# Layer 0 and 1 of a two-layer attention kernel: normalized tile written by ScalarE, a token-major feed-forward, mixing in three operations, stores two steps apart

## The chip, the cores and the metric

The kernel runs on one core of one Trainium2 chip. The metric is device time in microseconds, the median of several executions. Engines are named as in the profile: PE (TensorE matmul) and PEld (its weight loads), DVE (VectorE), ACT (ScalarE), POOL (GpSimd), SP (SyncE, which here only issues DMAs).

## The reference, cut to what matters

Two residual layers over x of shape (16, 512, 128), float32. Only layer 0's feed-forward branch and the normalization in front of both layers are touched.

```
xn = layernorm(x)                      # (x - mean) / sqrt(var + 1e-5), both layers
x  = x + attn(xn) + ffn(xn)            # 16 heads of 8, causal in layer 0

# ffn of layer 0
x_prev = concat([zeros, xn[:, :-1, :]])
xr = mu_r * xn + (1 - mu_r) * x_prev
xk = mu_k * xn + (1 - mu_k) * x_prev
r  = sigmoid(xr @ W_r.T)
out = r * (square(relu(xk @ W_k.T)) @ W_v.T)
```

## The kernel before, in words

One batch is 512 tokens, four tiles of 128 (NT = 4). Each layer is a software pipeline over the 16 batches, written as "bodies". A body has 64 slots: four groups u of heads, in each four key tiles kt, in each four tiles j (slot = 16u + 4kt + j). Every engine runs the same bodies in the same slot order with its own instructions, in order, and engines meet only through semaphores. First layer 0's bodies run alone, then three bodies of layer 0 and three of layer 1 interleaved slot by slot, then layer 1's alone.

In a slot PE makes transposed scores of one head and key tile (`scores_t`, L646, ring 0 of three PSUM banks), which ACT exponentiates into `probs` (L941), and the scores for the row maxima of a later group (`scores_max`, L667 and L671, mask added in L683; ring 1 of four PSUM banks), which DVE reduces into `maxs` (L1151 to L1182). At each kt, POOL masks (layer 0, L1290) or multiplies a bias (layer 1, L1316) on `probs`, and PE multiplies them with the values (`pv`, L630). POOL splits the maxima in two bf16 parts (`split_max`, L1299, L1301), PE transposes them (uses MT0 to MT3, L701), ACT copies them out (L839) and SP sends them as a row into the score operands (`stacks`, L506), which the next group's scores_t waits for.

All other work is put into slots by the hand-written tables `WORK_USES` (uses of a PSUM bank: slot of PE's part, slots later at which it is taken out, batch offset) and `OTHER_WORK` (slot, batch offset). A use claims the next bank of its ring in order and waits until the bank's last content has been taken; the names in `BY_DVE` use ring 1, all others ring 0. The parts that matter here:

- LN, slot 3: DVE takes bn_stats and bn_aggr of `x_tile` (L1064, L1068), adds eps (L1070). POOL makes `rstd` with pow one slot later (L1247).
- NORM, slot 7 in layer 0 and 18 in layer 1: DVE writes `xn` = (x - mean) * rstd, four operations (L1074). XT, slot 14 or 21: PE transposes xn (L707), ACT writes `xnT` (L842).
- MIX, slot 2, layer 0: DVE makes `fa` and `fb`, the two mixtures of `xnT` and `xnT` shifted by a token, two operations each (L1083, L1085).
- FR, slot 6, and FK, slot 9: PE multiplies W_r with fa and W_k with fb (L714), channels on the partitions. ACT takes tanh into `fc` (L851), relu into `fd` (L854). POOL squares fd (L1251).
- FV, slot 15: PE multiplies W_v with fd (L718); DVE takes it out a slot later as (fc + 1) * FV into fa (L1090). FT, slot 35: PE transposes fa back to tokens (L730); ACT scales it by 0.5 into `ffn` (L870).
- POST, slot 21: POOL adds residual, attention and `ffn` into `x_new` (L1256, L1258). STORE, slot 26 (layer 0) or 34 (layer 1): POOL moves the row indices on (L1230) and issues four indirect DMAs in a row (L1238).
- PJ0 to PJ3 project xnT to queries, keys and values (L724, L860); SQUARE, MEAN (slot 35), ROOT (slot 38) and SCALE_QK (slot 43) are the RMS norm of queries and keys (ACT L874 and L877, DVE L1094 to L1103). ACT loads another table for the square root and one to get back (L877, L941). QT (slot 47) and KT (slot 59) transpose q and k (L740); they are stored in parts (L533).
- SP, in order: at u = 0 the row of MT0, then the residual, then 24 loads of `stacks` from `parts_scratch` (L479; in layer 1 12 of them at u = 0 and 12 at u = 1, behind MT1); at u = 2, behind MT2, the next x_tile; at u = 3, behind MT3, the stores of parts. The maxima of the next body's first group, from slot 32 on, need the 24 loads.

Of the kernel before, what the change touches and what calls it, by code (L numbers as in the profile page):

```python
# [14 lines left out]
ALU = mybir.AluOpType  # L15
# [3 lines left out]
P = 128  # L19
NB, T, D = 16, 512, 128  # L20
H, HD = 16, 8
NT = T // P
# [31 lines left out]
BOTH = 3  # L54
ST_BANKS, MAX_BANKS = 3, 4
# [48 lines left out]
def place(layer, kt, j):  # L104

    if layer == 1:
# [20 lines left out]
    0: {"MIX": (2, 1), "LN": (3, 2), "NORM": (7, 2), "VALUES": (15, 1), "POST": (21, -1),  # L127
        "STORE": (26, -1), "SQUARE": (32, 2), "MEAN": (35, 2), "ROOT": (38, 2), "SCALE_QK": (43, 2)},
    1: {"LN": (3, 2), "NORM": (18, 2), "BESIDE": (22, -1), "STORE": (34, -1)},
# [174 lines left out]
def build(nc, a, out):  # L304
# [14 lines left out]
    with ExitStack() as ctx:  # L319
# [36 lines left out]
        rstd = sb("rstd", [P, NT])  # L356
        sqr = sb("sqr", [P, NT, 2 * P])
# [18 lines left out]
        mu = sb("mu", [P, 4])  # L376
# [180 lines left out]
        def _(pe):  # L557
# [39 lines left out]
            def body(B):  # L597
# [89 lines left out]
                def other(slot):  # L687
# [21 lines left out]
                    if layer == 0:  # L709
                        for n, name in enumerate(("FR", "FK")):  # L710
                            if B.due(name, slot):
                                work = claim(name)
# [13 lines left out]
                        if B.due("FT", slot):  # L726
                            work = claim("FT")
# [3 lines left out]
                            last.then_inc(full, 1)  # L731
# [81 lines left out]
        def _(act):  # L813
# [8 lines left out]
            def body(B):  # L822
# [8 lines left out]
                def other(slot):  # L831
                    u = slot // 16
                    mo, mu_ = (u + 1) // NG, (u + 1) % NG
                    if B.out(f"MT{u}", slot):
# [4 lines left out]
                        fn(mT[:], work[0:2 * G * NT, 0:P // 2].bitcast(BF16), ACT.Copy).then_inc(taken, 1)  # L839
                    if B.out("XT", slot):  # L840
# [7 lines left out]
                    if layer == 0:  # L848
# [17 lines left out]
                        if B.out("FT", slot):  # L866
                            work = filled("FT")
                            if B.has(-1):
                                act.wait_ge(s["post"], B.count(2, 2, -1))
                            fn(ffn[:, B.parity(1)].rearrange("p t d -> p (t d)"), work, ACT.Copy, scale=0.5  # L870
                               ).then_inc(taken, 1)
# [85 lines left out]
        def _(dve):  # L957
# [49 lines left out]
            def before_second_body():  # L1007
# [4 lines left out]
                v.tensor_scalar(mu[:, 2:4], mu[:, 0:2], -1.0, 1.0, ALU.mult, ALU.add).then_inc(rep_chain, 1)  # L1012
                dve.wait_ge(rep_chain, 5)

            def after_second_body():
# [5 lines left out]
                dve.wait_ge(rep_chain, 6)  # L1021
# [3 lines left out]
            def body(B):  # L1025
# [13 lines left out]
                def other(slot):  # L1039
# [21 lines left out]
                    if B.due("LN", slot):  # L1061
# [7 lines left out]
                        link(last, "ln", 3, 2, 2)  # L1069
# [132 lines left out]
        def _(pool):  # L1202
# [13 lines left out]
            def body(B):  # L1216
# [25 lines left out]
                def other(slot):  # L1242
                    if B.due("STORE", slot):
                        store()
# [130 lines left out]
```

## Time and profile before

| | us |
|---|---|
| three runs, median (lowest to highest) | 1820.95 (1817.0 to 1830.35) |
| the profiled execution, its own time | 1825.96 |
| its span, first to last instruction | 1824.1 |
| mean granted TensorE clock | 0.943 of full |
| busy over the span | PE 1606.0, DVE 1445.2, ACT 1287.8, POOL 932.1 |

Layer 0 alone runs steadily from about 120 to 826 us, both layers interleaved to about 1000 us, layer 1 alone to the end. The busy times are sums over stages with different limits. "PEclk" in the windows is the granted share of TensorE's full clock; a window half of which ran at the lower level shows 0.75. A row of windows gives the stretch, its length, the busy time of PE, PEld, DVE, ACT and POOL with their instruction counts, PEclk, the DMA share and GB/s.

### The profile page before, as it was taken

To read this page: it belongs to the slowest core of one execution; us is meant where nothing else is said; L and a number is where in the kernel's file an instruction comes from. 1 tells how busy PE (TensorE), PEld (TensorE's weight loads), DVE (VectorE), ACT (ScalarE), POOL (GpSimd) and SP (SyncE) were. 2 spreads that over 40 slices of the span, in tenths; PEclk is the share of its full clock that TensorE was granted. 3 is DMA by queue.
4 is the path that set the end of the run, shared out by engine and by line. 5 is a ranking of instruction groups with operands and counts; after the bars stand their busy time and mean duration, and the time that the engine had idled before them with its cause. 6 is when DMAs were issued, how large, how long until landed. Compare 5 with 4: busy or idle time off the path is not lost.

```text
span 1824.1 us, 32723 instructions
## 1 busy us (share of the span) xinstructions
PE 1606.0 (88%) x11594; PEld 621.3 (34%) x11594; DVE 1445.2 (79%) x2571; ACT 1287.8 (71%) x2502; POOL 932.1 (51%) x1144
## 2 busy tenths in 40 slices
PE   4798898888888888889879999999999999999995
PEld 2453333333333333333323233232332323323231
DVE  4358778787877878878878888888888888898881
ACT  1227777666766666777667788877888888887885
POOL 2123545554455444555455565555665556564555
PEclk9759989898999989999989999999999999999999
DMA  8313323222223222213232222322222222222200
GB/s 269 58 35 65 71 58 70 55 64 69 71 71 65 70 67 70 71 47 78 63 56 59 55 56 56 59 59 54 56 50 65 59 61 57 54 54 59 60 18 18
DMA packets 133122, 116.36 MB, mean 64 GB/s; under 512 B 16856, under 2 KB 125664, under 8 KB 132960
## 3 DMA queue, kind: packets, MB, share of 16 engines
q1 hardware_dynamic: 126272, 100.64, 23.7%
q0 software_dynamic: 4096, 8.40, 1.4%
q10 hardware_dynamic: 2592, 5.24, 0.9%
q8 instruction: 93, 1.52, 0.3%
q14 instruction: 69, 0.57, 0.1%
HBM read 79.63 MB, written 33.55 MB: 62 GB/s over the span
## 4 chain that ended last, share of the span: by engine, by line
PE 55%; DVE 21%; ACT 10%; issue 4%; DMA 4%; SPq 2%; POOL 2%; another core or an unknown queue 0%; POOLq 0%; ACTq 0%; DVEq 0%
PE pv_acc L630 15%; PE scores_transposed L646 12%; ACT probs L941 5%; PE scores_transposed L774 4%; PE scores_for_max L667 3%; PE scores_transposed L724 3%; DMA stacks<-parts_scratch 3%; DVE maxs L1151 3%; DVE maxs L1178 3%; DVE maxs L1182 2%; DVE xn L1074 2%; PE scores_transposed L746 2%; PE scores_for_max L671 2%; PE scores_for_max L782 2%; PE scores_for_max L683 2%
## 5 line engine op out<-in xcount | busy, mean ns | idle before, releaser
L941 ACT ACTIVATE probs<-scores_transposed 128x512 f32<-128x512 f32 x1664 | 908.9, 600 | 234.7 <-PE scores_transposed L646 221.2
L646 PE MATMUL scores_transposed<-stacks 62*128 62x512 bf16 (+3 forms) x2048 | 575.4, 347 | 61.7 <-ACT probs L941 36.9
L1316 POOL TENSOR_TENSOR probs<-probs,near_bias 128x512 f32<-128x512 f32 x256 | 324.8, 1272 | 360.1 <-ACT probs L941 359.8
L630 PE MATMUL pv_acc<-probs,vals 128*32 128x512 f32 (+3 forms) x4096 | 485.4, 547 | 18.4 <-issue 9.7
L1151 DVE TENSOR_REDUCE maxs<-scores_for_max 128x2 f32<-128x1024 f32 x340 | 409.2, 1221 | 77.9 <-PE scores_for_max L667 75.7
L646 PEld LDWEIGHTS scores_transposed<-stacks 62*128 62x128 bf16 x2048 | 150.5, 94 | 625.6 <-ACT probs L941 298.1
L667 PE MATMUL scores_for_max<-stacks 60*128 60x512 bf16 x1024 | 324.6, 385 | 15.0 <-DVE maxs L1151 8.4
L671 PE MATMUL scores_for_max<-stacks 60*128 60x512 bf16 (+3 forms) x1024 | 262.4, 315 | 37.1 <-DVE maxs L1179 27.0
L1182 DVE TENSOR_REDUCE maxs<-scores_for_max 128x1 f32<-128x512 f32 x256 | 175.0, 684 | 90.8 <-PE scores_for_max L683 79.4
L1154 DVE TENSOR_REDUCE maxs<-scores_for_max 128x1 f32<-128x512 f32 x344 | 226.4, 684 | 25.7 <-PE scores_for_max L667 23.0
L1290 POOL TENSOR_SCALAR_AFFINE_SELECT probs<-probs 128x512 f32<-128x512 f32 x256 | 166.9, 667 | 139.1 <-ACT probs L941 138.6
L1178 DVE TENSOR_REDUCE maxs<-scores_for_max 128x1 f32<-128x384 f32 x256 | 140.3, 548 | 70.3 <-PE scores_for_max L683 60.0
L683 PE MATMUL scores_for_max<-causal_halves,ident_halves 64*128 64x128 bf16 (+2 forms) x1280 | 193.3, 237 | 0.0
L630 PEld LDWEIGHTS pv_acc<-probs,vals 128*32 128x32 f32 x4096 | 82.8, 110 | 179.9 <-issue 135.8
L683 PEld LDWEIGHTS scores_for_max<-causal_halves,ident_halves 64*128 64x128 bf16 x1280 | 115.2, 99 | 39.3 <-issue 7.2
L1222 POOL TENSOR_TENSOR parts<-rest,parts 128x512 bf16<-128x512 f32 x64 | 75.4, 1178 | 67.0 <-ACT parts L917 67.0
L671 PEld LDWEIGHTS scores_for_max<-stacks 60*128 60x128 bf16 x1024 | 76.8, 95 | 56.0 <-DVE maxs L1179 32.9
L1173 DVE TENSOR_REDUCE maxs<-scores_for_max 128x2 f32<-128x512 f32 x128 | 87.4, 683 | 8.0 <-PE scores_for_max L683 7.0
L667 PEld LDWEIGHTS scores_for_max<-stacks 60*128 60x128 bf16 x1024 | 73.6, 93 | 41.1 <-DVE maxs L1151 24.3
L746 PE MATMUL scores_transposed<-xnT,w 128*128 128x512 f32 x128 | 78.9, 701 | 9.2 <-ACT probs L941 7.7
L1247 POOL TENSOR_TENSOR rstd<-mv,minus_half 128x4 f32<-128x4 f32 x32 | 40.2, 1256 | 71.5 <-DVE mv L1070 71.5
L1238 POOL DMA_INDIRECT out_dram<-x_new,slots_now x64 | 63.0, 985 | 23.8 <-issue 14.8
(129 smaller groups left out, 2031.4 us busy)
## 6 DMA issues: line engine op xcount, KB each, us to landing
stacks<-parts_scratch SPq DMA_DIRECT2D x768, 64.0 KB
parts_scratch<-parts SPq DMA_DIRECT2D x64, 384.0 KB, 2.6
x_tile<-in_L_attn_x_dram SPq DMA_DIRECT2D x16, 256.0 KB, 2.8
probs<-in_fc_B_dram ACTq DMA_DIRECT2D x1, 4096.0 KB, 19.1
stage_a<-in_fc_A_T_dram SPq DMA_DIRECT2D x1, 4096.0 KB, 16.9
stacks<-mT SPq DMA_DIRECT2D x256, 4.0 KB
x_res<-in_L_attn_x_dram SPq DMA_DIRECT2D x16, 256.0 KB, 3.6
x_tile<-x_between_layers SPq DMA_DIRECT2D x16, 256.0 KB
```

Of the source, the lines that this page charges most:

```text
L630: last = mm(acc[VW * j:VW * j + VW, q0:T], columns[:, first:first + VW], probs[:, row, column:column + width], start=(kt == 0 and pu % PAI ...
L646: last = mm(st[:, bank, column:column + T - q0], ks[p][rows, h, P * kt:P * kt + P], qs[p][rows, h, q0:T], start=True, stop=True)
L667: mm(bank, qs[p][rows, h, P * qt:P * qt + P], ks[p][rows, h, :], start=True, stop=True).then_inc(s["s1_ready"], 1)
L671: mm(bank[:, column:column + P * (qt + 1)], qs[p][rows, h, P * qt:P * qt + P], ks[p][rows, h, 0:P * (qt + 1)], start=True, stop=False, ski ...
L683: last = mm(masked, ident_halves[half, n, :], mask, start=False, stop=(n == 1), skip_group_check=True)
L941: fn(probs[:, row, :], st[:, B.use(("st", u, number)).bank, :], ACT.Exp, scale=SCALE).then_inc(s["exp_done"], 1)
L1151: v.reduce_max(maxs[:, su % 2, :].rearrange("p (e x) -> p e x", e=E)[:, :, column], s1[:, bank - 1:bank + 1, :], AX_X).then_inc(s["red_don ...
L1154: v.reduce_max(maxs[:, su % 2, column:column + 1], s1[:, bank, :], AX_X).then_inc(s["red_done"], 1)
L1178: v.reduce_max(maxs[:, su % 2, wide:wide + 1], bank[:, 0:3 * P], AX_X)
L1182: v.reduce_max(maxs[:, su % 2, column:column + 1], bank, AX_X).then_inc(s["red_done"], 1)
L1290: g.affine_select(out=diag, in_=diag, compare_op=ALU.is_ge, fill=0.0, base=0, pattern=[[0, G], [1, P]], channel_multiplier=-1).then_inc(s[ ...
L1316: g.tensor_tensor(diag, diag, near_bias[:, kt, :].unsqueeze(1).broadcast_to([P, G, P]), ALU.mult).then_inc(s["emul_pool"], 1)
```

## The change

The normalized tile is written by ACT as Identity(scale * x + bias), with scale = rstd and bias = -mean * rstd. DVE negates the mean, POOL multiplies it with rstd. NORM moves to slot 11 (layer 0) and 19 (layer 1). MIX becomes one difference into `fd` and one fused operation each for fa and fb; `mu` loses its two complement columns. FR and FV put the tokens on the partitions by using fa and fd as the stationary operand, in four matmuls of 128 columns each; so FT and its copy are gone, DVE writes `ffn` directly, and FV moves from slot 15 to 35. The factor 0.5 goes into W_v once, at set-up. Layer 0's OA is taken out a slot later, MT1 moves from slot 19 to 21; in layer 1 MT0 moves from 4 to 6, XT from 21 to 20, MT2 from 35 to 43. The four indirect stores are issued two slots apart in both layers. The diff, cut to its core:

```
+STORE_STEPS = 2
 WORK_USES = {
-    0: {"MT0": (2, 0, 0), "FR": (6, 0, 1), "FK": (9, 0, 1), "XT": (14, 0, 2), "FV": (15, 0, 1),
-        "OA": (16, 0, -1), "MT1": (19, 0, 0), ... "FT": (35, 0, 1), ...
-    1: {... "MT0": (4, 0, 0), ... "XT": (21, 0, 2), ... "MT2": (35, 0, 0), ...
+    0: {"MT0": (2, 0, 0), "FR": (6, 0, 1), "FK": (9, 0, 1), "XT": (14, 0, 2), "OA": (16, 1, -1),
+        "MT1": (21, 0, 0), ... "FV": (35, 0, 1), ...
+    1: {... "MT0": (6, 0, 0), ... "XT": (20, 0, 2), ... "MT2": (43, 0, 0), ...
 OTHER_WORK = {
-    0: {... "NORM": (7, 2), ...     1: {... "NORM": (18, 2), ...
+    0: {... "NORM": (11, 2), ...    1: {... "NORM": (19, 2), ...
@@ PE
-        for n, name in enumerate(("FR", "FK")):
-                pe.wait_ge(s["mix_done"], B.count(4, 2 * n + 2, 1))
-                mm(work, wrkv[:, n, :], (fa, fb)[n][:], start=True, stop=True).then_inc(full, 1)
+        if B.due("FR", slot):
+            pe.wait_ge(s["mix_done"], B.count(3, 2, 1))
+            for t in range(NT):
+                last = mm(work[:, P * t:P * t + P], fa[:, P * t:P * t + P], wrkv[:, 0, :], ...)
+        if B.due("FK", slot):
+            pe.wait_ge(s["mix_done"], B.count(3, 3, 1))
+            mm(work, wrkv[:, 1, :], fb[:], start=True, stop=True).then_inc(full, 1)
         if B.due("FV", slot):
-            mm(work, wrkv[:, 2, :], fd[:], start=True, stop=True).then_inc(full, 1)
+            for t in range(NT):
+                last = mm(work[:, P * t:P * t + P], fd[:, P * t:P * t + P], wrkv[:, 2, :], ...)
-        if B.due("FT", slot):
-            taken_out("FV")
-            for t in range(NT):
-                last = tr(work[:, P * t:P * t + P], fa[:, P * t:P * t + P], ident[:])
@@ ACT
+        if B.due("NORM", slot):
+            act.wait_ge(s["pow_ln"], B.count(2, 2, 2))
+            for t in range(NT):
+                fn(xn[:, t, :], x_tile[:, t, :], ACT.Identity, scale=rstd[:, t:t + 1],
+                   bias=shift[:, t:t + 1]).then_inc(s["xn_done"], 1)
-        if B.out("FT", slot):
-            fn(ffn[:, B.parity(1)]..., work, ACT.Copy, scale=0.5).then_inc(taken, 1)
@@ DVE
+        v.tensor_scalar(mv[:, :, 0], mv[:, :, 0], -1.0, None, ALU.mult)
         v.tensor_scalar(mv[:, :, 1], mv[:, :, 1], LN_EPS, None, ALU.add).then_inc(s["ln"], 1)
-        for t in range(NT):
-            v.tensor_scalar(xn[:, t, :], x_tile[:, t, :], mv[:, t, 0:1], rstd[:, t:t + 1], ...)
         if B.due("MIX", slot):
+            link(v.tensor_tensor(fd[:], xt[:, 1:T + 1], xt[:, 0:T], ALU.subtract), "mix_done", 3, 1, 1)
             for n, mix in enumerate((fa, fb)):
-                link(v.tensor_scalar(mix[:], xt[:, 1:T + 1], mu[:, n:n + 1], None, ALU.mult), ...)
-                v.scalar_tensor_tensor(out=mix[:], in0=xt[:, 0:T], scalar=mu[:, 2 + n:3 + n], in1=mix[:], ...)
+                v.scalar_tensor_tensor(out=mix[:], in0=fd[:], scalar=mu[:, n:n + 1], in1=xt[:, 0:T], ...)
         if B.out("FV", slot):
-            v.scalar_tensor_tensor(out=fa[:], in0=fc[:], scalar=1.0, in1=work, op0=ALU.add, op1=ALU.mult)
+            dve.wait_ge(s["post"], B.count(2, 2, -1))
+            v.scalar_tensor_tensor(out=ffn[:, B.parity(1)]..., in0=fc[:], scalar=1.0, in1=work, ...)
@@ POOL
+    for t in range(NT):
+        if B.after("STORE", slot, STORE_STEPS * t):
+            store_rows(t)
     if B.after("LN", slot, 1):
         g.tensor_tensor(rstd[:], mv[:, :, 1], half[:, 0:NT], ALU.pow).then_inc(s["pow_ln"], 1)
+        pool.wait_ge(s["pow_ln"], B.count(2, 1, 2))
+        g.tensor_tensor(shift[:], mv[:, :, 0], rstd[:], ALU.mult).then_inc(s["pow_ln"], 1)
@@ set-up, DVE
-    v.tensor_scalar(mu[:, 2:4], mu[:, 0:2], -1.0, 1.0, ALU.mult, ALU.add)
+    v.tensor_scalar(wrkv[:, 2, :], wrkv[:, 2, :], 0.5, None, ALU.mult)
```

## Rows read from the trace of the kernel before

**Rows 1.** DVE timeline: first token-mixing instruction of the batches at 169 and 813 us.
```profile
169.44 0.76 DVE L1083 TENSOR_SCALAR fa<-xnT,mu 128x512 f32<-128x512 f32 x1
...
812.66 0.77 DVE L1083 TENSOR_SCALAR fa<-xnT,mu 128x512 f32<-128x512 f32 x1
```

**Rows 2.** Windows: one steady layer 0 stretch, then both layers, then layer 1 (PEclk is 1.00 at full clock).
```profile
413.90:512.84 98.94, 86.41 (x756) 37.09 (x756) 78.75 (x174) 68.40 (x126) 50.52 (x75) 0.93 0.24 66
...
826.00:1000.00 174.00, 152.34 (x1084) 56.72 (x1088) 143.00 (x243) 121.77 (x244) 84.51 (x107) 0.92 0.30 64
1000.00:1824.10 824.10, 753.66 (x4833) 250.79 (x4825) 688.37 (x993) 655.10 (x1322) 471.17 (x494) 0.98 0.23 53
```

**Rows 3.** Waits of PE, 150 to 800 us (layer 0): total us, times, longest.
```profile
PE scores_for_max L671 <- DVE maxs L1179: 26.3, 27, 1.5
PE scores_transposed L701 <- POOL msp L1301: 15.2, 20, 1.1
PE scores_transposed L646 <- ACT probs L941: 11.3, 7, 1.7
...
PE pv_acc L630 <- POOL probs L1290: 5.9, 13, 0.5
```

**Rows 4.** Critical chain, 455 to 512 us: start, us, what.
```profile
464.76 0.70 DVE fa L1083
...
466.91 0.75 DVE fb L1085
...
470.92 2.42 DVE xn L1074 x4
...
475.98 1.95 PE scores_for_max L718 x2
...
489.49 0.74 issue
```

**Rows 5.** Windows around the three drops of the granted clock in two batches.
```profile
421.00:431.00 10.00, 8.48 (x50) 3.30 (x44) 6.48 (x14) 3.38 (x7) 2.82 (x6) 0.66 0.39 120
449.00:455.00 6.00, 5.00 (x34) 2.24 (x34) 3.75 (x8) 4.41 (x9) 4.34 (x6) 0.72 0.01 3
471.00:481.00 10.00, 8.03 (x62) 3.53 (x61) 7.83 (x18) 4.64 (x10) 3.59 (x7) 0.83 0.56 119
```

**Rows 6.** Groups by line: busy us, mean ns, idle before.
```profile
L1074 DVE TENSOR_SCALAR xn<-x_tile,mv,rstd 128x128 f32<-128x128 f32 x128 | 65.5, 638 | 2.3 <-POOL rstd L1247 2.3
L905 ACT ACTIVATE ffn<-scores_transposed 128x128 f32<-128x128 f32 x64 | 17.8, 278 | 17.2 <-PE scores_transposed L774 17.2
L730 PE MATMUL scores_transposed<-ident,fa 128*128 128x128 f32 x64 | 11.0, 296 | 0.0
L764 PE MATMUL scores_transposed<-wqkv,xnT 128*128 128x128 f32 x128 | 19.5, 297 | 0.0
L1090 DVE SCALAR_TENSOR_TENSOR fa<-fc,scores_for_max 128x512 f32<-128x512 f32 x16 | 11.0, 685 | 16.0 <-PE scores_for_max L718 16.0
L1230 POOL TENSOR_TENSOR slots_now<-slots_now,a_batch 128x4 int32<-128x4 int32 x30 | 5.9, 197 | 0.0
L877 ACT ACT_TABLE_LOAD x16 | 20.5, 1283 | 0.3
```

**Rows 7.** Timelines of POOL and DVE, batch of 462 us: stores, a mask, means.
```profile
484.65 1.07 POOL L1238 DMA_INDIRECT x_between_layers<-x_new,slots_now  x1 [0.29 <-POOL slots_now L1230]
...
489.52 0.65 POOL L1290 TENSOR_SCALAR_AFFINE_SELECT probs<-probs 128x512 f32<-128x512 f32 x1
...
493.76 1.21 DVE L1094 TENSOR_REDUCE ssq<-sqr 128x128 f32<-128x1024 f32 x1
```

**Rows 8.** Waits of PE, 826 to 1000 us (both layers), then 1000 to 1700 (layer 1).
```profile
PE scores_transposed L707 <- DVE xn L1074: 6.0, 2, 3.3
...
PE scores_transposed L646 <- ACT probs L941: 14.4, 46, 0.6
```

**Rows 9.** Critical chain, 1155 to 1212 us (layer 1).
```profile
1164.05 7.78 DMA stacks<-parts_scratch
```

More of the change, by code:

```diff
@@ L126 @@
 OTHER_WORK = {
-    0: {"MIX": (2, 1), "LN": (3, 2), "NORM": (7, 2), "VALUES": (15, 1), "POST": (21, -1),
+    0: {"MIX": (2, 1), "LN": (3, 2), "NORM": (11, 2), "VALUES": (15, 1), "POST": (21, -1),
         "STORE": (26, -1), "SQUARE": (32, 2), "MEAN": (35, 2), "ROOT": (38, 2), "SCALE_QK": (43, 2)},
-    1: {"LN": (3, 2), "NORM": (18, 2), "BESIDE": (22, -1), "STORE": (34, -1)},
+    1: {"LN": (3, 2), "NORM": (19, 2), "BESIDE": (22, -1), "STORE": (34, -1)},
 }
@@ L356, in build @@
         rstd = sb("rstd", [P, NT])
+        shift = sb("minus_mean_rstd", [P, NT])
         sqr = sb("sqr", [P, NT, 2 * P])
@@ L375, in build @@
         wrkv = sb("wrkv", [P, 3, P])
-        mu = sb("mu", [P, 4])
+        mu = sb("mu", [P, 2])
         normw = sb("normw", [P, 2, HD])
@@ L709, in other @@
                     if layer == 0:
-                        for n, name in enumerate(("FR", "FK")):
-                            if B.due(name, slot):
-                                work = claim(name)
-                                pe.wait_ge(s["mix_done"], B.count(4, 2 * n + 2, 1))
-                                mm(work, wrkv[:, n, :], (fa, fb)[n][:], start=True, stop=True).then_inc(full, 1)
+                        if B.due("FR", slot):
+                            work = claim("FR")
+                            pe.wait_ge(s["mix_done"], B.count(3, 2, 1))
+                            for t in range(NT):
+                                last = mm(work[:, P * t:P * t + P], fa[:, P * t:P * t + P], wrkv[:, 0, :],
+                                          start=True, stop=True)
+                            last.then_inc(full, 1)
+                        if B.due("FK", slot):
+                            work = claim("FK")
+                            pe.wait_ge(s["mix_done"], B.count(3, 3, 1))
+                            mm(work, wrkv[:, 1, :], fb[:], start=True, stop=True).then_inc(full, 1)
                         if B.due("FV", slot):
@@ L717, in other @@
                             pe.wait_ge(s["kact_done"], B.count(1, 1, 1))
-                            mm(work, wrkv[:, 2, :], fd[:], start=True, stop=True).then_inc(full, 1)
+                            for t in range(NT):
+                                last = mm(work[:, P * t:P * t + P], fd[:, P * t:P * t + P], wrkv[:, 2, :],
+                                          start=True, stop=True)
+                            last.then_inc(full, 1)
                         for t in range(NT):
@@ L865, in other @@
                                ).then_inc(s["vals_done"], 1)
-                        if B.out("FT", slot):
[L867 to L871, printed above, removed]
                         if B.due("SQUARE", slot):
@@ L1069, in other @@
                         link(last, "ln", 3, 2, 2)
+                        v.tensor_scalar(mv[:, :, 0], mv[:, :, 0], -1.0, None, ALU.mult)
                         v.tensor_scalar(mv[:, :, 1], mv[:, :, 1], LN_EPS, None, ALU.add).then_inc(s["ln"], 1)
-                    if B.due("NORM", slot):
-                        dve.wait_ge(s["pow_ln"], B.count(1, 1, 2))
-                        for t in range(NT):
-                            v.tensor_scalar(xn[:, t, :], x_tile[:, t, :], mv[:, t, 0:1], rstd[:, t:t + 1],
-                                            ALU.subtract, ALU.mult).then_inc(s["xn_done"], 1)
                     for side, name in enumerate(("QT", "KT")):
@@ L1236, in store, with store_rows @@
                         pool.wait_ge(s["dve_taken"], B.use("PR").taken[1])
-                    for t in range(NT):
-                        g.indirect_dma_start(x_dst[layer],
-                                             bass.IndirectOffsetOnAxis(slots_now[:, layer, t:t + 1], 0),
-                                             x_new[:, t, :], None).then_inc(s["x_stored"], 16)
+                def store_rows(t):
+                    g.indirect_dma_start(x_dst[layer], bass.IndirectOffsetOnAxis(slots_now[:, layer, t:t + 1], 0),
+                                         x_new[:, t, :], None).then_inc(s["x_stored"], 16)
                 def other(slot):
```

16 lines of the change are left out of this document (5 added, 11 removed), and 12 rows, old and new, of the table WORK_USES.

## The prediction

> **What bounds the kernel now.** I read the views in this order: the windows by stage, the waits of PE, the critical chain of one layer 0 batch, the granted clock in fine windows, then the groups by line for prices.
>
> The windows split the span in three. In layer 0 no engine is full: over two batches PE is busy 86.41 of 98.94 us, DVE 78.75, at a mean granted clock of 0.93. In layer 1 PE is busy 753.66 of 824.10 us at 0.98, so it is close to its limit [rows 2]. So layer 0 has the room. Its period is (812.66 - 169.44) / 13 = 49.48 us a batch [rows 1].
>
> The waits say who makes PE stand: in 13 batches 26.3 us for maxima that DVE had not reduced, 15.2 us for split maxima, 11.3 us for exponentials, 5.9 us for POOL's masks [rows 3]. The chain shows where: DVE is on it from 464.76 to 467.66 us with the mixing, and with the four operations that write `xn`, 2.42 us; as soon as these are through, PE transposes xn and then runs FV, two passes in 1.95 us [rows 4]. That FV is slow because the granted clock falls right there: half the clock, 1.2 GHz of the two levels 1.2 and 2.4, follows the stretch in which PE stood waiting for DVE. The reader is to see three drops in two batches: 0.66 over 10 us, 0.72 over 6 and 0.83 over 10, that is 2 x (1 - clock) x length = 6.8, 3.4 and 3.4 us at half clock [rows 5]. The first and third follow the `xn` stretch, the second the pair of table loads for the root.
>
> **The change part by part**, against the profiled execution (1825.96 us, of which 1824.1 span; the median of the runs is 5.0 lower). Layer 0 has 13 full batches between 169 and 813 us.
>
> *NORM to ACT, layer 0.* DVE loses 2.42 us on the chain [rows 4] and gets one small operation, at most 0.2 us by the nearest small row, POOL's 128x4 [rows 6]. POOL gets one more of that size plus a wait on itself, 0.3 us; behind it in POOL's order is the mask that pv at slot 12 waits for, a wait of 5.9 / 13 = 0.45 us now [rows 3]. DVE reaches LN earlier by what mixing saves (0.5 or more, below), so that mask comes 0 to 0.45 us earlier: I take 0.3. The longest single wait of PE on DVE is 1.5 us, once a batch, right behind `xn` [rows 3]; DVE arrives about 3 us earlier there, so it goes. Sum 1.8 us. ACT pays: an activation of 128x128 takes 278 ns [rows 6], four of them at most 1.1 us with nothing overlapped and 0.6 if starts overlap; I take 0.85. It lies at slot 11, ahead of XT at 14, and behind it in ACT's queue stand the exponentials of slot 12 and the copy of pv_acc that pv at slot 16 waits for. ACT is busy 68.40 of 98.94 us [rows 2], and 4.64 of 10 us around this place [rows 5], so I cost it at nothing; without that cover it is 0.85 a batch. What is late next is XT itself: LN, pow, shift, four activations end within some 0.1 us of when PE can be there.
>
> *The clock.* With the stand gone, the drops behind it should go: 10.2 us at half clock in two batches [rows 5], 5.1 a batch, of which half is lost, 2.55 us. PE is the one waited for in most of it. Bounds 0 and 2.55; I take 2.0, since one of the drops may move to another stand instead of going.
>
> The Trainium skill has a rule against this ("TensorE: Matmul & The Clock Gate", section Part 4: PE-mode transpose): transposes do not count as work for the clock. By it the four of XT would leave the clock low whatever precedes them, and this term would be 0. The drop that follows the table loads has no such transposition in front, which speaks for the idle time; no row separates the two at XT. It is the first rival.
>
> *MIX in three.* 2.9 us now for four operations [rows 4]; three, at 0.69 (a fused one of this size, L1090 [rows 6]) to 0.8 each, are 2.1 to 2.4: 0.5 to 0.8 less. It is inside the same DVE backlog as `xn` and already spent there; nothing of its own.
>
> *FR and FV by tokens, FT away.* Four f32 matmuls of 128 columns cost 19.5 us / 16 = 1.22 a batch (the layer 1 row L764), the one of 512 columns 1.95 / 2 = 0.98 at full clock [rows 4, 6]. So each of the two pays 0 to 0.24 more. FT's four transposes go, 11.0 / 16 = 0.69 us of PE [rows 6], and its copy on ACT, about 0.5. FV leaves the stretch where PE is the bound (1 us at full clock) and comes to slot 35, in front of the only long stand of PE that remains, that for ACT's table loads (11.3 us in 7 cases, up to 1.7 us [rows 3]). Bounds 0.2 and 1.2; I take 0.6.
>
> *FV on DVE.* The operation is the same, 685 ns, and loses its idle time of 1 us in front at slot 16 [rows 6], which was not the bound. At slot 36 it stands directly behind MEAN, 1.21 us plus two more [rows 7], and holds one of four ring 1 banks meanwhile; reductions behind it, and SCALE_QK and QT after them, come up to 0.6 us later. Cost 0 to 0.8, taken 0.6.
>
> *Stores two slots apart.* They block POOL from 484.65 to the mask at 489.52 us [rows 7], and PE stands 0.74 us until that mask is done [rows 4]. The mask can now run after the first of them: a gain of 0 to 0.74, taken 0.7. The other three, 1.3 us each, lie between later masks; the fourth, at slot 32, is behind the split of maxima and not in front of it. OA and MT1 one and two slots later have slack of ten slots, no cost.
>
> Together 1.8 + 2.0 + 0.6 - 0.6 + 0.7 = 4.5 us a batch, 13 batches: 58.5 us.
>
> *Both layers, 826 to 1000 us.* XT waited 6.0 us for `xn` in two places [rows 8]. ACT, less laden there than DVE (121.77 against 143.00 us [rows 2]), should end most of it: 4 us, bounds 0 and 6.
>
> *Layer 1.* DVE loses at most (65.5 - 13 x 2.42) / 19 = 1.8 us a batch (what is left of the group [rows 4, 6], start-up included), ACT gets 0.85 at slot 19, in front of XT at slot 20. PE waits 14.4 us in 12 batches for exponentials [rows 8], so ACT matters as much as DVE. Moreover the 24 stack loads are on the chain: 7.78 us in one piece of DMA, issued behind MT1 at slot 17, which does not move, and needed at slot 32 [rows 9]. What is won between those slots is given back there. MT0 and MT2 later by 2 and 8 slots keep the five-slot lead that MT3 has. Bounds -8 and +8 over 14 batches; I take 1 us less.
>
> Sum: 58.5 + 4 + 1 = 63.5, so 1825.96 - 63.5 = 1762.5 for such an execution and 1820.95 - 63.5 = 1757.5 for the median.
>
> **The rivals.**
> *The clock stays low at XT.* For it: XT and idle time always come together in this trace. Against it: a batch has six groups of transposes (XT, OA, FT, QT, OB, KT), and two batches show three drops in all [rows 5]. Then the 2.0 us fall away: 2.5 x 13 + 5 = 37.5, giving 1783.
> *The wait moves.* XT waits for ACT instead of DVE, or the stack loads, which layer 0 also needs by slot 32, bind once the batch shortens by five. For it: pow, shift and NORM are a chain over three engines. Against: layer 0 issues all 24 loads at u = 0, sixteen slots ahead of layer 1's second half, and its waits show none of PE on them [rows 3]. Only some 1 us a batch remains, about 13 us and 0 to 5 more: 1806.
> *Slower: Identity needs a table of its own.* Then each of 32 NORMs costs ACT two loads of 1283 ns [rows 6] at slot 11 or 19. In layer 0 the present pair already makes PE stand up to 1.7 us [rows 3]; this eats the gain of 1.8 and keeps the clock low, leaving 0.7 x 13 = 9 us. In layer 1, with PE at 91%, a stand of 1.6 and a drop of 1.7 us in each of 14 batches are 46 us more: 1820.95 - 9 + 46 = 1858. It decides from one load in front of NORM on. Against: it is the root's line that has the 16 loads [rows 6], once a batch, though copies, squares and tanh come between the exponentials too. The Trainium skill ("ScalarE: Activation LUTs", Table sets: the hidden batching unit) says identity is in every set, and would give this case no time at all.
> *More than forecast.* All upper bounds, 5.9 a batch, and 14 in the rest: 1730.
>
> **How the numbers follow.** Forecast as stated (1736 to 1776) 0.60, more than forecast 0.08, clock stays low 0.17, the wait moves 0.10, slower 0.05. The range leaves out one in ten on each side: 1731 to 1800. A measurement here tells about 1% (18 us) from no change: faster by more 0.85, within 1% 0.10, slower 0.05.
>
> **What would show it.** The windows of layer 0: period 45 us instead of 49.5, mean clock 0.97 or more, one drop in two batches instead of three. In the waits, L671 on DVE from 26 to below 10 us, a small new one of L707 on ACT. No ACT_TABLE_LOAD on NORM's line. Layer 1's part of the span within 8 us of 824. The forecast is wrong if XT is followed by half clock as before, if L707 waits over 0.5 us a batch, or if the period stays above 47.

## The result, and the profile after

The changed kernel takes 1796.75 us (1790.92 to 1801.12, four runs) against 1821.31 us (four runs beside it): a ratio of 0.9857, 95% interval 0.9827 to 0.9888. It is faster by 24.6 us; the forecast was 63.5. Its median is within the range given, near the upper end, so the range held and the forecast did not. The profiled executions (1790.92 us, span 1789.2, against 1825.96, span 1824.1) are 35.0 us apart. The first lies 6 us below its median, the second 5 us above, so 10 us of that gap are scatter. Ratios leave out slow executions, those over 1.5% above the fastest of their kernel (three of ten in e9, three of six in e13, two of six in e17), and medians do not, so these three ratios are 0.3 to 0.7% lower than their medians say.

The windows of the changed kernel, over two of its batches, over the steady part of layer 0, around two drops of the clock, and around one XT (columns as in [rows 2]):

```profile
405.33:498.50 93.17, 83.42 (x780) 38.92 (x772) 73.42 (x165) 70.33 (x133) 52.59 (x77) 0.93 0.29 70
170.00:780.00 610.00, 543.22 (x5045) 252.59 (x5046) 478.96 (x1079) 458.93 (x863) 341.09 (x494) 0.94 0.29 70
434.00:444.00 10.00, 8.65 (x61) 4.11 (x61) 7.39 (x17) 6.83 (x14) 6.36 (x8) 0.66 0.00 0
480.00:490.00 10.00, 8.28 (x62) 3.58 (x62) 7.39 (x17) 6.59 (x12) 6.09 (x7) 0.66 0.00 0
411.00:421.00 10.00, 9.16 (x86) 4.13 (x87) 6.79 (x16) 8.23 (x18) 6.93 (x12) 1.00 0.57 117
```

The same 610 us of the kernel before:

```profile
170.00:780.00 610.00, 531.73 (x4647) 228.24 (x4643) 485.61 (x1068) 418.97 (x774) 308.84 (x453) 0.93 0.27 67
```

and of the run e2 below, the kernel before with NORM alone moved:

```profile
170.00:780.00 610.00, 539.13 (x4960) 236.23 (x4952) 485.91 (x1099) 464.97 (x879) 333.64 (x498) 0.97 0.28 70
```

The first row answers to the first of [rows 2]: two batches in 93.17 us instead of 98.94. PE is busy 83.42 instead of 86.41 us and stands 9.75 instead of 12.53. The clock is what did not follow: 0.93 in both pairs of batches, 0.94 against 0.93 over 610 us. The drops have changed their place. Both of the pair in the third and fourth row (0.66 over 10 us, 6.8 us at half clock each) lie behind the table loads of the root, where [rows 5] had one of three. None lies at XT any more: in the last row XT runs at full clock.

The timeline of DVE after gives the period, as [rows 1] did:

```profile
168.74 1.00 DVE L1083 SCALAR_TENSOR_TENSOR fa<-fd,mu,xnT 128x512 f32<-128x512 f32 x1
...
775.97 1.00 DVE L1083 SCALAR_TENSOR_TENSOR fa<-fd,mu,xnT 128x512 f32<-128x512 f32 x1
```

(775.97 - 168.74) / 13 = 46.71 us a batch against 49.48, where 45 was forecast. That is 2.77 x 13 = 36 us, all of the 35 us between the two profiled executions. The rest of the kernel, where 5 us were expected, gave nothing.

The waits of PE in layer 0 after, to be laid beside [rows 3]:

```profile
PE scores_transposed L648 <- ACT probs L945: 16.4, 15, 1.4
PE scores_transposed L703 <- POOL msp L1305: 15.5, 17, 1.1
PE scores_for_max L673 <- DVE maxs L1178: 11.6, 14, 1.0
PE scores_transposed L709 <- ACT xn L848: 10.9, 14, 1.4
...
PE scores_for_max L745 <- DVE big L1102: 6.1, 14, 0.8
PE scores_transposed L648 <- DMA stacks<-mT: 4.1, 1, 4.1
```

The wait for unreduced maxima is down from 26.3 to 11.6 us. Against it stand a new one, 10.9 us of XT on ACT's `xn`, and one that has grown, 6.1 us of QT on DVE's scaling (0.9 before, from 170 to 780 us). One batch stood 4.1 us for the row of maxima that SP sends behind MT1. The group of ACT's line 848 (busy us, mean ns, idle time before) and the critical chain at one NORM show why XT waits:

```profile
L848 ACT ACTIVATE xn<-x_tile,minus_mean_rstd,rstd 128x128 f32<-128x128 f32 x128 | 52.4, 484 | 0.1
```

```profile
410.66 0.59 ACT probs L945
411.25 1.53 ACT xn L848 x4
412.79 0.14 issue
412.92 0.63 PE scores_transposed L709 x4
```

One activation with two per-partition operands takes 484 ns, not the 278 it was priced at, and a NORM of four 52.4 / 32 = 1.64 us, not 0.85. PE is ready for XT at about 412.2 us and gets it at 412.9. And before QT, the timeline of DVE after:

```profile
429.36 0.69 DVE L1089 SCALAR_TENSOR_TENSOR ffn<-fc,scores_for_max 128x512 f32<-128x512 f32 x1 [0.27 <-PE scores_for_max L727]
429.96 1.21 DVE L1093 TENSOR_REDUCE ssq<-sqr 128x128 f32<-128x1024 f32 x1
...
435.40 1.22 DVE L1102 TENSOR_TENSOR big<-big,rrms 128x1024 f32<-128x1024 f32 x1
```

FV's operation with its wait (0.95 us) stands in front of MEAN here, not behind it: in its entry (35, 0, 1) the second number, 0, is the number of slots later, so it is taken out in its own slot 35. The same holds for the (15, 0, 1) of the kernel before: it was taken out in slot 15, not a slot later.

Layer 1's waits of PE, 1000 to 1700 us, beside [rows 8]:

```profile
PE scores_transposed L648 <- ACT probs L945: 11.7, 38, 0.6
PE scores_transposed L709 <- ACT xn L848: 10.6, 12, 0.9
```

ACT's exponentials hold PE a little less than before, but XT now waits 0.9 us in nearly every batch (12 waits). Before, PE had no wait for `xn` in the list of layer 1.

### The profile page after: what moved, and what is told of

It reads as the page before. It is cut to its first block, busy times and chain, and to the rows that moved or that the text cites. A ratio compares the mean times of both kernels' runs of the same rounds, so it can differ in the third digit from the quotient of the medians.

```text
span 1789.2 us, 32996 instructions
## 1 busy us (share of the span) xinstructions
PE 1579.5 (88%) x11722; PEld 631.3 (35%) x11722; DVE 1387.0 (78%) x2459; ACT 1326.8 (74%) x2614; POOL 952.5 (53%) x1176
## 3 DMA queue, kind: packets, MB, share of 16 engines
q1 hardware_dynamic: 126272, 100.64, 24.6%
## 4 chain that ended last, share of the span: by engine, by line
PE 61%; DVE 17%; ACT 11%; issue 4%; DMA 3%; POOL 2%; SPq 2%; POOLq 0%; ACTq 0%; DVEq 0%
PE pv_acc L632 17%; PE scores_transposed L648 14%; ACT probs L945 6%; PE scores_transposed L779 4%; PE scores_for_max L669 3%; PE scores_transposed L735 3%; DVE maxs L1150 3%; ACT xn L848 2%; PE scores_for_max L685 2%; PE scores_transposed L751 2%; PE scores_for_max L787 2%; PE scores_for_max L673 2%; PE scores_for_max L698 2%; DVE maxs L1181 2%; DVE maxs L1177 2%
## 5 line engine op out<-in xcount | busy, mean ns | idle before, releaser
L669 PE MATMUL scores_for_max<-stacks 60*128 60x512 bf16 x1024 | 328.3, 387 | 9.2 <-DVE maxs L1150 5.9
L673 PE MATMUL scores_for_max<-stacks 60*128 60x512 bf16 (+3 forms) x1024 | 257.2, 316 | 17.3 <-DVE maxs L1178 11.6
L1294 POOL TENSOR_SCALAR_AFFINE_SELECT probs<-probs 128x512 f32<-128x512 f32 x256 | 178.5, 710 | 159.9 <-ACT probs L945 159.6
```

Of the source, the lines that this page charges most:

```text
L669: mm(bank, qs[p][rows, h, P * qt:P * qt + P], ks[p][rows, h, :], start=True, stop=True).then_inc(s["s1_ready"], 1)
L673: mm(bank[:, column:column + P * (qt + 1)], qs[p][rows, h, P * qt:P * qt + P], ks[p][rows, h, 0:P * (qt + 1)], start=True, stop=False, ski ...
L1294: g.affine_select(out=diag, in_=diag, compare_op=ALU.is_ge, fill=0.0, base=0, pattern=[[0, G], [1, P]], channel_multiplier=-1).then_inc(s[ ...
```

## The experiments

Every run has its own executions of the kernel before beside it (medians 1819.5 to 1825.1), so the ratio is what is compared. "Period" is that of layer 0 as above; "layer 1" is the mean over twelve batches between copies of xnT (before 56.65 us, changed 56.92). Rows of waits are those of PE in the 610 us from 170 us on, unless said otherwise, with total, count and longest. "Half clock" is 2 x (1 - clock) x length over the same 610 us (before 85 us, changed 75). Period, layer 1, waits and half clock are those of the one profiled execution of each kernel. The half clock differs between executions of one kernel: over the whole span the four of e6 lie between 146 and 202 us.

**One part against the rest.**

`e1_norm_on_dve`: the changed kernel with the old NORM.

```
-        if B.due("NORM", slot):
-            act.wait_ge(s["pow_ln"], B.count(2, 2, 2))
...
+        if B.due("NORM", slot):
+            dve.wait_ge(s["pow_ln"], B.count(1, 1, 2))
...
```

> The changed kernel with NORM back on DVE at its old slots (7 and 18, XT at 21 in layer 1); all else stays changed. Theory A (the predicted terms): NORM on DVE costs a stand of 1.8 us and 2 us of clock a batch in layer 0, so about 1797 + 13 x 3 to 4 = 1836 to 1850. Theory B (XT now waits 0.8 us a batch for ACT in both layers, and the clock falls once a batch at the root's table loads anyway): layer 0 loses 1 to 1.5 us a batch, layer 1 wins 0.9 x 14: 1797 + 16 - 12 = about 1800, with the layer 1 wait of L709 gone.

Measured: 1808.62 us, ratio 0.9918 (0.9882 to 0.9954). Period 49.0, layer 1 56.3; PE waits 29.1 us for maxima again and never for xn.

`e2_norm_on_act_alone`: the same edit the other way round, on the kernel before.

> The kernel before with NORM alone moved to ACT (slots 11 and 19, XT at 20 in layer 1). Theory A: this carries 1.8 + 2.0 us a batch: 1821 - 50 = 1771. Theory B: it gives 1 to 1.5 us a batch in layer 0 and takes 0.9 in layer 1: 1810 to 1821. The four activations should take 1.64 us in one piece, as in the changed kernel.

Measured: 1800.85 us, ratio 0.9889 (0.9856 to 0.9922). Period 46.52, layer 1 57.0, half clock 41 us.

In the profiled executions NORM alone gives layer 0 all of its gain: 46.5 against 46.7 with everything. By the medians it gives most: e2's profiled execution is the fastest of its eight, 9 us below their median. NORM on ACT costs layer 1 some 0.3 us a batch (57.0 against 56.65), and putting it back wins 0.6 there (56.3 against 56.9). Theory A, the predicted terms, had 1836 to 1850 and 1771 and is out in both; theory B had the layer 1 side right, and its 1 to 1.5 us for layer 0 was too small (49.0 - 46.7 = 2.3, and 49.5 - 46.5 = 3.0).

`e9_feed_forward_alone`: the kernel before with FR and FV by tokens, FV at 35 and FT gone, as the change has them:

```
-        ..., "FV": (15, 0, 1), ... "FT": (35, 0, 1), ...
+        ..., "FV": (35, 0, 1), ...
```

> The kernel before with the token-major feed-forward alone: FR and FV by tokens, FV at 35, FT gone; NORM, mixing, stores and slots as before. As predicted it saves 0.6 us of PE a batch and costs 0.6 on DVE: period 49.5, total within 5 us of before. Theory D: FV on DVE in front of the sums makes PE wait at QT (L740 on DVE, 0.9 us in all before, now 5 or more), and less half clock is won than lost; PE's busy time at full clock falls by 0.7 to 0.9 us a batch. Total 1815 to 1821.

Measured: 1814.08 us, ratio 0.9921 (0.9878 to 0.9964), so 0.5% faster by the medians and 0.8% by the ratio, a little more than both theories allowed. Its period is 48.85, in an execution 9 us above the median. The wait for the scaling appears as theory D said:

```profile
PE scores_for_max L742 <- DVE big L1102: 4.4, 12, 0.6
```

Alone it is worth 0.8%, NORM alone 1.1%, and everything together 1.4%. The gains seem not to add, but the intervals are too wide to show it.

`e6_stores_in_a_row`, the changed kernel with

```
-STORE_STEPS = 2
+STORE_STEPS = 0
```

> The changed kernel with its four indirect stores issued one after the other again, at slots 26 and 34. If the predicted 0.7 us a batch is right: pv waits 0.7 us for the mask in layer 0 again, period 46.3 to 47.0, about 9 us more in all. If the freed time is given back at the next wait: period unchanged, total within 3 us.

Measured: 1792.28 us, ratio 0.9843 (0.9765 to 0.992), not distinguishable from the changed kernel. Period 46.49, also not longer, although pv's wait is back, now with no releaser found:

```profile
PE pv_acc L632 <- issue: 6.2, 13, 0.5
```

So a stand of 0.5 us a batch is there, where 0.7 was predicted. Whether removing it gains anything is not shown: the interval is 28 us wide and holds both no change and the 9 us of the forecast, and this execution has 31 us less at half clock than the changed kernel's.

**The clock and the stand before QT.** The root's operation was replaced in both kernels by one that needs no other table; the root itself is left out.

```
-                            fn(rrms[:], ssq[:], ACT.Sqrt).then_inc(s["root_done"], 1)
+                            fn(rrms[:], ssq[:], ACT.Tanh).then_inc(s["root_done"], 1)
```

`e3_changed_no_root_table`:

> The changed kernel with the square root of the RMS norm replaced by a tanh, so that the root itself is left out (wrong scale of queries and keys) and no second table is needed. Theory B (the pair of table loads makes PE stand and the clock falls behind it in every batch): two loads a batch of 1.28 us go, the drops behind them (5.1 us at half clock a batch) go: layer 0 period from 46.7 to 42 to 43, in all 1797 - 16 x 4 = 1733, clock in layer 0 0.99. Theory C (the clock falls wherever PE stands at all, here at XT): period 45, clock 0.95 or lower, in all about 1772.

`e4_before_no_root_table`:

> The kernel before with the same replacement (the root is left out). Theory B: the stretch of xn on DVE still makes the clock fall once a batch, so the gain is smaller than in the changed kernel: the table stand of about 1.6 and one drop of 3.4 in two batches: 1821 - 16 x 2.4 = 1783. If it gains as much as the changed kernel does, the two stands are independent of one another and theory B falls.

Measured: 1791.74 us, ratio 0.9805 (0.9734 to 0.9876), for the changed kernel, and for the one before 1821.79, ratio 1.0016 (0.9982 to 1.0051). Two loads a batch are worth nothing in the kernel before and little, if anything, in the changed one, whose intervals with and without them overlap (periods: changed 46.3, before 49.0). The wait has passed to the other engine, here in the changed kernel:

```profile
PE scores_for_max L745 <- DVE big L1102: 24.2, 13, 1.9
```

24.2 us in 13 batches for DVE's scaling, against 5.5 with the loads in place over the same stretch (in e4 22.3 in 12, against 0.9). PE stands before QT for two chains of about one length, ACT's loads and DVE's sums, reciprocal and scaling, so taking away one shows the other. Theory B's 1733 is far off.

`e11_root_on_pool` tried to shorten both: one power -0.5 on POOL for reciprocal, root and loads. `e12_root_on_pool_fv_52` has FV at slot 52 too.

```
-                            v.reciprocal(ssq[:], ssq[:]).then_inc(s["rms"], 1)
-                            fn(rrms[:], ssq[:], ACT.Sqrt).then_inc(s["root_done"], 1)
+                            g.tensor_tensor(rrms[:], ssq[:], half[:], ALU.pow).then_inc(s["root_done"], 1)
```

> The changed kernel with reciprocal (DVE), square root (ACT) and both table loads replaced by one power -0.5 on POOL. Theory F (PE stands before QT for two chains at once, ACT's table loads and DVE's FV, sums and reciprocal; only when both shorten does the stand shrink, which is why leaving out the root's table alone gave little): both stands go if POOL's 128x128 power takes 2 us or less: period 46.3 to about 43.5, half clock below 25 us, 1797 - 40 = 1757. If POOL needs 4 us or more, PE waits for the scaling instead and the total rises above 1797.

> As the run before, with FV at slot 52, so that DVE's chain in front of QT is 0.95 us shorter too. Theory F: a further 0.3 to 0.6 us a batch, 1750; if POOL's power is the bound, the same as the run before.

Measured: 2068.52 us (ratio 1.1379) and 2075.05 (1.1417).

The group of the new line in e11:

```profile
L1251 POOL TENSOR_TENSOR rrms<-ssq,minus_half 128x128 f32<-128x128 f32 x16 | 333.0, 20812 | 90.9 <-DVE ssq L1093 90.9
```

The power of 128x128 takes 20.8 us. In both, pv waits up to 20.2 us at a time for masks queued behind it. Theory F, that the stand shrinks only when both chains do, stays untested.

**Where FV stands.** `e5_fv_at_29`, the changed kernel with

```
-        "MT2": (32, 0, 0), "FV": (35, 0, 1), ...
+        "FV": (29, 0, 1), "PJ3": (31, 0, 2), "MT2": (32, 0, 0), ...
```

> The changed kernel with FV at slot 29 instead of 35, a stretch in which PE is full and DVE stands idle for 1 to 1.4 us at a time. Theory D (in the changed kernel FV's operation on DVE, 0.95 us with its wait, stands in front of the sums, the reciprocal and the scaling of q and k, and PE waits for those at QT, 5.5 us in 13 batches, with the clock falling behind it): the wait of L745 on DVE goes, the half clock in layer 0 (75 us) falls to about 40, period 46.5 to 45.5, in all about 12 to 15 us less. Rival E (place of FV does not matter, PE's sum of work does): period unchanged at 46.3.

Measured: 1797.1 us, ratio 0.985 (0.9794 to 0.9906): no change. The wait of QT on DVE is gone from the list, but half clock rose to 82 us and the period to 47.6. Theory D had its wait right and its gain wrong. The clock falls at XT again, in 11 of 13 batches, 37.5 us in all, here once:

```profile
468.00:478.00 10.00, 10.00 (x71) 3.90 (x71) 5.45 (x13) 6.37 (x13) 5.76 (x9) 0.83 0.39 99
```

Yet XT's transposes and its wait for ACT (9.6 us in 13) are those of the changed kernel, in which no drop lies there.

**How long NORM sits on ACT.** The next runs change that piece or what waits for it. `e7_xt_later`:

```
-"XT": (14, 0, 2)   (layer 0)      "XT": (20, 0, 2)   (layer 1)
+"XT": (17, 0, 2)                  "XT": (22, 0, 2)
```

> The changed kernel with XT three slots later in layer 0 (17) and two later in layer 1 (22). NORM on ACT takes 1.64 us, twice what was predicted, and PE waits 0.74 us in layer 0 and 0.8 in layer 1 a batch for it. Theory B: both waits go, 0.7 x 13 + 0.8 x 13 = 20 us less, 1777. Rival: ACT's 1.64 us delay its exponentials, and the wait comes back as one of L648 on ACT: total unchanged.

Measured: 1789.07 us, ratio 0.9785 (0.9702 to 0.9868), period 46.9, layer 1 56.4. In layer 0 the rival holds: XT no longer waits, and pv waits for masks instead, twice a batch; POOL makes them from ACT's exponentials, which stand behind NORM in ACT's queue:

```profile
PE pv_acc L632 <- POOL probs L1294: 20.8, 26, 1.1
```

That is 20.8 us against 6.2 in the changed kernel over the same stretch. In layer 1, 0.5 us a batch came, though XT still waits there (10.1 us in 12, now for exponentials). `e8_fv_at_52_xt_later` adds `"FV": (52, 0, 1)` in place of `(35, 0, 1)`:

> The changed kernel with XT later as in the run before and FV at slot 52, far behind the scaling. If theories B and D both hold, their gains add: 20 + 12 to 15 us less than the changed kernel, about 1763, half clock in layer 0 at 40 us or below.

Measured: 1787.59 us, ratio 0.9789 (0.9731 to 0.9848), the same again. Half clock was 48 us, not the 40 or below that was expected, and the time was 25 us above the expectation.

`e10_norm_one_operation` leaves the normalization out (a plain copy under the same name) and measures its price; `e15_norm_four_plain` keeps the four operations and drops only scale and bias:

```
-                        for t in range(NT):
-                            fn(xn[:, t, :], x_tile[:, t, :], ACT.Identity, scale=rstd[:, t:t + 1],
-                               bias=shift[:, t:t + 1]).then_inc(s["xn_done"], 1)
+                        fn(xn[:], x_tile[:], ACT.Identity).then_inc(s["xn_done"], NT)
```

> The changed kernel with NORM as one ACT operation of 128x512 that only copies x (the normalization itself is left out): about 0.63 us instead of 1.64. Theory B (the size of NORM on ACT is what PE waits for at XT, 0.74 and 0.8 us a batch): L709's wait falls to below 0.1 us a batch in both layers, about 0.7 x 29 = 20 us less, 1777. Rival: the loop closes elsewhere and less than 8 us comes of it.

> The changed kernel with its four activations without scale and bias operands (the normalization itself is left out). If the two per-partition operands make them slow: four in about 0.9 us, and the total near the run with one operation, 1746 to 1755. If the four instructions do: 1.6 us again and 1797.

Measured: 1745.76 us, ratio 0.9603 (0.9558 to 0.9649), and 1758.98, ratio 0.9652 (0.961 to 0.9695).

The groups of NORM's line in e10 and in e15:

```profile
L847 ACT ACTIVATE xn<-x_tile 128x512 f32<-128x512 f32 x32 | 20.1, 627 | 0.2 <-issue 0.2
```

```profile
L848 ACT ACTIVATE xn<-x_tile 128x128 f32<-128x128 f32 x128 | 28.8, 303 | 0.1
```

One operation of 627 ns, or four plain ones of 303 ns each: of the 484 ns, some 180 are the price of the two per-partition operands. With 1 us less on ACT the layer 0 period is 45.3 and layer 1 takes 55.5; the wait at XT is gone in e10 and nearly so in e15 (one of 0.6 us in layer 0, 1.6 us in 9 in layer 1). By the ratios 0.9857 and 0.9603 the 32 NORMs give 46 us, 1.4 us for each us taken from ACT, where its time had been costed at nothing. A part of that is the clock, as the part on the prediction says.

**A version that beats both.** `e13_layer1_norm_on_dve` leaves NORM on ACT in layer 0 and gives it to DVE in layer 1 (slot 18, XT at 21). `e14_norm_split` gives ACT two tiles and DVE two, in both layers; `e16_norm_split_fv_52` has FV at slot 52 too. The split:

```
+    0: {..., "NORM": (11, 2), "NORM_DVE": (9, 2), ...}
+    1: {..., "NORM": (19, 2), "NORM_DVE": (18, 2), ...}
...
-                        for t in range(NT):
+                        for t in range(2):
...
+        if B.due("NORM_DVE", slot):
+            dve.wait_ge(s["pow_ln"], B.count(2, 2, 2))
+            for t in range(2, NT):
+                v.tensor_scalar(xn[:, t, :], x_tile[:, t, :], rstd[:, t:t + 1], shift[:, t:t + 1],
+                                ALU.mult, ALU.add).then_inc(s["xn_done"], 1)
```

> The changed kernel with layer 1's NORM back on DVE (slot 18, XT at 21), layer 0's on ACT. If the ACT piece costs layer 1 what its waits show (0.8 us a batch at XT, against none with DVE): 56.9 to 56.3 us a batch there, 7 to 12 us less in all, about 1787. Rival (layer 1 is indifferent): within 3 us of the changed kernel.

> The changed kernel with tiles 0 and 1 normalized by ACT and 2 and 3 by DVE (slot 9 in layer 0, 18 in layer 1). If the length of the piece on ACT sets the loss: L709's wait gone in both layers, and about half of the 51 us of the run with one operation: 1770 to 1775. Rival (DVE's two operations, up to 1.2 us beside POOL, bring its backlog back): L673 on DVE above 1.2 us a batch, total at or above 1790.

> The split of NORM together with FV at slot 52, behind the scaling of q and k instead of in front. If both effects hold: 3 to 8 us less than the split alone, about 1767, and the lowest of all full kernels. If the stand before QT is ACT's alone: the same as the split.

Measured: 1784.4 us, ratio 0.9745 (0.9681 to 0.9809); 1776.86, ratio 0.976 (0.9731 to 0.9789); 1779.75, ratio 0.9769 (0.9739 to 0.98). Layer 1 takes 56.1, 55.8 and 56.2 us a batch, all below both kernels. The split is clearly ahead of the changed kernel (0.9857, 0.9827 to 0.9888), although layer 0 keeps a wait at XT, now for DVE's half (rows of e14):

```profile
PE scores_transposed L709 <- DVE xn L1078: 9.0, 13, 0.7
PE scores_transposed L648 <- DMA stacks<-mT: 6.9, 3, 4.5
```

`e17_split_mt1_at_19` and `e18_split_3_1` go after these two rows, from e14 on:

```
e17: -"MT1": (21, 0, 0)        +"MT1": (19, 0, 0)
e18: the same, and
     -for t in range(2):       +for t in range(3 - layer):       (ACT)
     -for t in range(2, NT):   +for t in range(3 - layer, NT):   (DVE)
```

> The split of NORM (tiles 0 and 1 on ACT, 2 and 3 on DVE) with MT1 back at slot 19 in layer 0. If MT1's move makes the stands for the row of maxima: L648 on DMA stacks<-mT from 7 us to 1, total 1777 - 5 = 1772. Rival (the row queues behind the 24 stack loads whenever the batch is short, wherever MT1 stands): the stands stay, total 1777 within 3.

> As the run before, with layer 0's NORM as three tiles on ACT and one on DVE (layer 1 stays two and two). XT is reached when the slower of both is through: ACT's three need 1.25 us, DVE's one 0.6, against 0.85 and 1.2: if DVE is the later one, L709's wait in layer 0 falls from 0.7 to about 0.4 us a batch, 4 us less; if ACT is, it stays and the total too.

Measured: 1776.31 us, ratio 0.9696 (0.9639 to 0.9752), and 1769.6, ratio 0.9724 (0.9694 to 0.9754).

Two rows of waits, of e17 first, then of e18:

```profile
PE scores_transposed L648 <- DMA stacks<-mT: 1.1, 3, 0.6
```

```profile
PE scores_transposed L648 <- DMA stacks<-mT: 7.1, 4, 4.0
...
PE scores_transposed L709 <- ACT xn L848: 4.2, 12, 0.4
```

With MT1 at 19 the stand for the row is 1.1 us in one run and 7.1 in the other, so its slot does not decide it. By the medians e17 takes what e14 takes, as the rival said. With three tiles on ACT XT's regular wait halves in layer 0, from 9.0 to 4.2 us, but one batch stands 2.1 us for DVE's tile. Of the complete kernels e18 has the lowest median, 1769.6 us; its interval overlaps that of e14, so only the split as such is shown, not its proportion.

## Why the prediction was wrong

**Right.** DVE's `xn` was what made PE stand: the wait for maxima fell by (26.3 - 11.6) / 13 = 1.1 us a batch, with no single wait above 1.0 us, and the drops at XT went with it. The other 0.7 of the 1.8 us did not come, and the wait for masks did not fall (5.9 us in 13 before, 6.2 in 13 after, from 170 to 780 us). No table load came with Identity, so the slower rival fell at once; the Trainium skill's sentence ("ScalarE: Activation LUTs", Table sets: the hidden batching unit) and this trace agree. FT's and FV's matmuls: PE's busy time fell by (86.41 - 83.42) / 2 = 1.5 us a batch, of which 0.6 is clock (below), so 0.9 of work where 0.6 was said.

**The step that failed first: the clock.** The forecast took 2.0 us a batch, on the ground that the drops go with the stand in front of XT and at most one moves. At XT that was right. Of the 85 us at half clock of the kernel before, 58 lie in 11 drops that begin at XT, and 27 in 7 drops behind the root's table loads. In the changed kernel none lies at XT. What failed is the rest: behind the stand before QT, which the prediction had called the only long one left, there are now 13 drops in 13 batches, 68 us instead of 27. The 610 us hold 12.3 batches before and 13.1 after, so half clock fell from 85 / 12.3 = 6.9 to 75 / 13.1 = 5.7 us a batch: by 1.2 us, worth 0.6 at the forecast's half, not 2.0.

All executions say the same. Span and clock of each give the time at half clock over the whole span: 204 us on the mean of 63 executions of the kernel before, 188 on that of the four changed ones. The 16 us between them are to be laid beside 2 x 2.0 x 13 = 52. The price of a half holds. Among those 63, half clock goes from 181 to 227 us and the time from 1809 to 1835 us, and a straight line through them rises by 0.49 us for each us. Through e6's four (146 to 202 us, 1784 to 1807 us) it rises by 0.40; the four of the changed kernel (169 to 200 us) show no such rise. This is what goes together in executions of one program, not an experiment on the clock. By it the clock gave some 8 us of the 24.6, and 26 had been taken.

The first rival falls. In 6 of the 11 drops at XT the clock had fallen 0.3 to 0.6 us before the first transposition. A window and PE's timeline of the kernel before show one:

```profile
423.00:423.60 0.60, 0.31 (x1) 0.10 (x1) 0.60 (x3) 0.00 (x0) 0.00 (x0) 0.60 0.55 176
```

```profile
423.29 0.50 PE L671 MATMUL scores_for_max<-stacks 60*128 60x384 bf16 x1 [1.52 <-DVE maxs L1179]
423.72 1.11 PE L707 MATMUL scores_transposed<-ident,xn 128*128 128x128 f32 x4
```

Moreover the drops went in the changed kernel although its transposes stayed. The Trainium skill ("TensorE: Matmul & The Clock Gate", Part 4: PE-mode transpose) says that transposes do not count as busy in the same way. That four of them alone keep the clock low was the rival's reading, and this trace goes against it at this place. What does decide is known in part only. The four kernels whose layer 0 has all of NORM on DVE (before, e1, e4, e9) have 9 to 12 drops at XT each. Of the 14 with half of it or more on ACT (e11 and e12 left out), 13 have none or one. The 14th is e5, with 11 at the same stand as in the changed kernel. Its drops begin 0.9 to 1.0 us after XT's first transposition, so for e5 the transposes are not excluded as a part of the cause.

**The term that was mis-sized: NORM on ACT**, taken as 0.85 us in a gap and costed at nothing. It takes 1.64 us, and XT waits 10.9 / 14 = 0.8 us a batch in layer 0 and 0.9 in layer 1. The nearest row was an activation from PSUM without such operands. The word "cover" failed too: ACT is idle there by the window, but what is queued behind the piece is the exponentials, which the masks and pv wait for (e7), and in e10 a microsecond less of it went with 1.4 us. Of e10's 46 us the clock has a share: its four executions have 134 us at half clock on the mean, 54 less than the changed kernel's 188. At 0.4 to 0.5 us each that is an estimate of 22 to 27 us, so about half of the 46 is left for ACT's time itself.

**Layer 1 and the part with both layers**, 5 us expected, 0 measured: the DVE time freed was not what PE waited for, the ACT time added was (e1, e13).

**FV on DVE and the stores.** FV was put one slot too late in the working; it stands before MEAN, and QT's wait rose by 0.4 us a batch where 0.6 was charged. Of the stores' 0.7 us a stand of 0.5 exists (e6), and what removing it is worth stays open. MIX in three takes 2.7 us on the mean (0.99 + 0.97 + 0.74), not 2.1 to 2.4, which no term rested on. MT1's later slot was costed at nothing; stands of up to 4.1 us for its row came, but e18 has them with the old slot, so their cause is open.

By the books of the two 610 us windows, a batch: stands 1.9 forecast, 1.2 measured (78.27 / 12.3 = 6.3 and 66.78 / 13.1 = 5.1); work 0.6 and 0.9; clock 2.0 and 0.6. The sum is 2.8 against 4.5, 22 us of the miss of 39. Layer 1 with the part before it is some 6 us more, and 10 us are the scatter of the profiled executions about their medians. The upper bounds of the prediction add up to 1.8 + 2.55 + 1.2 + 0.74 = 6.3 a batch, not 5.9, which would put its last rival at 1725.

The rivals come out so: "the wait moves" was the nearest in its mechanism (XT on ACT), with 1806; "the clock stays low" in its effect, with 1783, though not in its cause. The measured 1796.75 lies between them, which fits both having happened in part. Of the prediction's own signs of being wrong one came: XT waits 0.8 us a batch, above 0.5. What stays open is what sets the number of drops (41 to 82 us among runs with nearly one period, and 11 drops at XT in e5), and whether shortening both chains before QT would pay.

## What to carry to other kernels

Moving work off the engine that is waited for is only half a sum: price the new piece at its exact form and operands, and ask what is queued behind it on the new engine, since an idle share says nothing about that. When a stand was removed here, the drops at it went, and drops behind the next long stand became more. Time at half clock scatters by tens of us between executions of one kernel and takes about half of itself along (0.49 in 63 executions), so compare it over all executions, not over two profiled ones. Splitting the moved piece between the two engines beat both placements here.

## What the runs showed of the hardware

An activation of 128x128 with scale and bias from SBUF takes 484 ns, 303 ns without them, and one of 128x512 without them 627 ns. The same normalization on DVE, in the kernel before, takes 332 to 349 ns a tile in all 66 cases in which POOL was idle. In those 30 in which POOL was busy throughout it takes 617 to 662 ns or about 1090 ns, and twice, at the start, over 8 us. A power on POOL takes 1.25 us for 128x4 on the mean and 20.8 us for 128x128, that is (20.8 - 1.25) / 124 = 0.16 us for each further column. A pair of table loads a batch can cost nothing at all when another chain ends at the same point (e4).
